# Block probabilities scaled by reciprocal sums: sixteen ScalarE multiplications per tile in place of one GpSimd pass

## The chip, the cores and the metric

The kernel runs on one core of a Trainium2 chip. The metric is the device time of one execution in microseconds (us); less is better. The engines' names in the profile are PE (TensorE; PEld is its weight load), ACT (ScalarE), DVE (VectorE), POOL (GpSimd) and SP (SyncE, which here issues nearly all DMAs).

## What is computed

A transformer layer on x of 2 x 1024 tokens of 256 channels, in fp32: x = layernorm(x + attention(x)), then x = layernorm(x + x Wt + bias), Wt a weight rounded to three levels. The attention has 16 heads of 128 channels and two branches that share one query. Cut to what matters here:

```python
q = rmsnorm(rope(h @ Wq_c @ Wq_up), q_norm_w)            # 16 heads
ck = rmsnorm(h.reshape(b, 64, 16 * 256) @ W_comp, k_norm_w)   # one key (and value) per block of 16 tokens
valid = blk_end[None, :] < pos[:, None]
c_out = softmax([where(valid, q @ ck / sqrt(128), -1e30), sink])[..., :-1] @ ck
s = 50 * tanh(q @ k_sw / sqrt(128) / 50)                 # window of the last 64 tokens
sw_out = softmax([where(window, s, -1e30), sink])[..., :-1] @ v_sw
ao = c_out + sw_out
attention = (ao by 4 groups of heads @ Wg) @ Wo
```

The change is in the normalisation of the block branch: exponentials divided by their sum (the sum takes in the sink).

## The kernel before

**Set-up.** Before the loop the kernel transposes x, makes keys, values and block keys, and multiplies the weights together, so that in the loop the attention's output goes straight from the heads to 256 channels: Weff is Wg times Wo per head (f16, high and low part), and CW is the block values times Weff, 16 heads by 8 blocks = 128 rows to a chunk.

**The loop.** The 2048 tokens are 16 tiles of 128, numbered 0 to 15; a tile is one step `i` of `all_steps` (L339) for its middle part (`mid`). Software pipelining runs four stages in one step: the query of tile i+1 (`front`), the scores and softmax of tile i (`mid`), the output projection and first layernorm of tile i-1 (`proj`), the feed-forward part of tile i-2 (`ffn`). Each engine has its own program of this loop, in an order written out by hand; all ordering between engines is by semaphores. There is no planner. The number of block groups is `groups(i)` = i mod 8 + 1: tile 0 and 8 see 8 blocks at most, tiles 7 and 15 see 64.

**The block probabilities.** For a tile, TensorE writes the block scores of all heads to banks 4 and 5 (L603). VectorE takes the maxima (L1056, `mn`, signal `d_cmax`). ScalarE exponentiates head by head, 16 times (L831), into the tile `Ec` of 128 partitions x (64 blocks x 16 heads), heads innermost, so that one head is a column with a stride of 16 floats; each exponential has its maximum as bias (a pointer to a 128x1 column) and sums its row into `sc` through the accumulator (a second instruction, ACTIVATION_READ_ACCUMULATOR). `Ec` is a part of `room_h`, `sc`, `rc` and `mn` are parts of `room_K`. VectorE's `divide(0)` (the normalisation of the window branch's first half, L1095 to L1114) also takes the reciprocals `rc` of the sums (L1105, signal `d_rc`). GpSimd then multiplies `Ec` by `rc`, one TENSOR_TENSOR over (8 groups - 1) x 16 elements (L1242, signal `g_cn`). TensorE waits for `g_cn` (L690), and at the very end of its step transposes the chunks of `Ec` with `probs_T` (L684, 1 to 8 transposes, signal `p_ct`), after a wait for `d_ql` too (L692). ScalarE copies them out of PSUM to `PcT` (L850, printed at L706 as `room_wo<-PS`, signal `a_ct`), and the next step's `project_blocks` multiplies them with CW (L623).

**The order on each engine, around the change, in one step i with all stages on:**

- TensorE: `queries(i+1)` in two halves, the second one waiting for `a_ct` of the step before (L477); window scores of tile i (L589), which wait for the transposed query by DMA (`s_qt`); x1 transposes (L560); block scores (L599, L603); feed-forward (L568); `project_blocks` (L623) and most of `project_high` (L632); `values(0)` (L666), which waits for GpSimd's mask and for the block exponentials; the rest of L632; `project_low` (L639); `values(1)` (L666); then `probs_T` (L684).
- ScalarE: second square of the query of tile i+1 (L775); four tanh (L816) with a small copy between (`room_h<-PS` at L706); two exponentials of the window branch (L822); 16 block exponentials (L831); the query's high part, twice (`room_K<-PS` at L706), then `output_high(0)` (`ao<-room_wg` at L706); the wait for `p_ct` and the `PcT` copy; the first square of tile i+2 (L775); `output_high(1)` (`ao<-room_wg`).
- VectorE: sums of squares (L1030, L1032), rope (L1045, L1046, L1076), maxima (L1056), query times its norm (L1085), `divide(0)` (L1101, L1105, L1107, L1112), the query's low part twice (L1121, signal `d_ql`), the first layernorm (L1135 to L1147), `divide(1)` (L1101, L1107, L1112).
- GpSimd: a power for the query's norm (L1223), two masks (L1217), the final result of an older tile (L1228), the pass of the change (L1242), `output_low(0)` (L1207), a power and two passes of the first layernorm (L1249, L1253, L1257), `output_low(1)` (L1207).
- SyncE: the queries' transposing DMAs (L370), then the outputs' (L379), high part of both halves before the low part, then the stored result (L397).

On ScalarE, before the change, these lines stand one behind the other:

```python
output_high(0)
act.wait_ge(p_ct, i + 1)
n = groups(i)
narrow(PcT[:, 0:n, :], bank(2, 2)[:, 0:n * P].rearrange("p (a q) -> p a q", q=P), a_ct)
```

Of the kernel before, what the change touches and what calls it, by code (L numbers as in the profile page):

```python
# [8 lines left out]
HEADS, D, QC = 16, 128, 64  # L9
# [4 lines left out]
P = 128  # L14
# [32 lines left out]
def build(nc, h, wqc, wqup, wk, wv, wcomp, qnw, knw, sink, wg, wo, fw, fb, rope_t, block_t, window_t, out):  # L47
# [8 lines left out]
    with ctx:  # L56
# [8 lines left out]
        def sem(name):  # L65
            return ctx.enter_context(nc.semaphore(name))
# [101 lines left out]
        def bank(b, n=1):  # L168
# [28 lines left out]

        a_sq, a_tanh, a_es, a_ec, a_qt, a_ct, a_at, a_xt = (sem(n) for n in (  # L200
            "a_sq", "a_tanh", "a_es", "a_ec", "a_qt", "a_ct", "a_at", "a_xt"))

        d_nq, d_nl, g_rs = sem("d_nq"), sem("d_nl"), sem("g_rs")
        d_red, d_qn, d_rope, d_add, d_cmax, d_rc, d_ql, d_ao, d_fr, d_y, d_xl = (sem(n) for n in (
            "d_red", "d_qn", "d_rope", "d_add", "d_cmax", "d_rc", "d_ql", "d_ao", "d_fr", "d_y", "d_xl"))

        g_mask, g_cn, g_al, g_rl, g_x1, g_xb, g_out = (sem(n) for n in (
            "g_mask", "g_cn", "g_al", "g_rl", "g_x1", "g_xb", "g_out"))
        s_out, s_qt, s_ah, s_al = sem("s_out"), sem("s_qt"), sem("s_ah"), sem("s_al")
        s_chain = sem("s_chain")  # L210

# [17 lines left out]
        def groups(t):  # L229

            return t % TPB + 1
# [170 lines left out]
        def _(pe):  # L402
# [145 lines left out]
            def step(i, front, mid, proj, ffn):  # L548
# [138 lines left out]
                        last.then_inc(p_ct, 1)  # L687

                if mid:
                    pe.wait_ge(g_cn, i + 1)  # L690
                    if front:
                        pe.wait_ge(d_ql, 2 * i + 4)  # L692
                    probs_T(0)
                    probs_T(1)
# [5 lines left out]
        def _(act):  # L700
# [92 lines left out]
            def step(i, front, mid, proj, ffn):  # L793

                def feed_forward_high():

                    act.wait_ge(p_xt, i - 1)
                    narrow(x1T[:, 0, :, :], x1_bank(mid).rearrange("p (k n) -> p k n", k=KC), a_xt)

                if front and i < 1:  # L800
                    square(i + 1, 0)
                if front:
                    square(i + 1, 1)
                if ffn and not mid:
                    feed_forward_high()
                if i == -1:
                    output_weights()
                if i == 0:
                    act.wait_ge(s_fw, 1)
                if mid:  # L810
                    for u, b in enumerate((6, 4, 5, 6)):
                        c, hf = divmod(u, 2)
                        if hf == 0:
                            wait(act, g_mask, 2 * i + c - 1)
                        act.wait_ge(p_sw, 4 * i + u + 1)
                        nc.scalar.activation(E[:, c, 8 * hf:8 * hf + 8, :], bank(b).rearrange("p (a q) -> p a q", q=WIN),  # L816
                                             ACT.Tanh, scale=1.0 / CAP).then_inc(a_tanh, 1)
                        if ffn and u == 0:
                            feed_forward_high()
                    for c in range(2):  # L820
                        act.wait_ge(a_tanh, 4 * i + 2 * c + 2)
                        nc.scalar.activation(E[:, c, :, :], E[:, c, :, :], ACT.Exp, scale=CAP).then_inc(a_es, 1)  # L822
                if mid:
                    if i == 0:
                        evac(G_FT, wfT[:, :, :], two(G_FT))

                    act.wait_ge(d_cmax, i + 1)
                    wait(act, p_ct, i)
                    n = SUB * groups(i)
                    for hd in range(HEADS):  # L830
                        last = nc.scalar.activation(Ec[:, 0:n, hd], bank(4 + hd // 8)[:, (hd % 8) * n:(hd % 8 + 1) * n], ACT.Exp,  # L831
                                                    bias=mn[:, hd:hd + 1], accum_out=sc[:, hd:hd + 1])
                        if hd % 8 == 7:
                            last.then_inc(a_ec, 1)
                if front and i >= 0:
                    query_high(i + 1, 0)
                    query_high(i + 1, 1)
                if i == -1:
                    value_weights(act, lambda dst, src: nc.scalar.mul(dst, src, v_unit), 0)
                if mid:  # L840
                    def output_high(c):

                        act.wait_ge(d_ao, 2 * i + c + 1)
                        wait(act, s_ah, 64 * i)
                        narrow(ao16[:, 0, c, :, :], ao[:, c, :, :], a_at)

                    output_high(0)
                    act.wait_ge(p_ct, i + 1)
                    n = groups(i)
                    narrow(PcT[:, 0:n, :], bank(2, 2)[:, 0:n * P].rearrange("p (a q) -> p a q", q=P), a_ct)  # L850
                    if i + 2 < NT:
                        square(i + 2, 0)
                    output_high(1)
# [5 lines left out]
        def _(dve):  # L859
# [164 lines left out]
            def step(i, front, mid, proj, ffn):  # L1024
# [65 lines left out]
                def divide(c):  # L1090

                    dve.wait_ge(p_pv, 2 * i + c + 1)

                    full = bank(4, 4).rearrange("p (k x) -> p k x", x=1024)[:, :, 0:3 * VW].rearrange("p k (n d) -> p k n d", d=VW)
                    third = bank(5)[:, 0:2 * VW].rearrange("p (n d) -> p n d", d=VW)  # L1095

                    def split(x):
                        return x[:, 0:6].rearrange("p (k n) -> p k n", k=2), x[:, 6:8]

                    for pv, d, e in zip((full[:, :, :, D], third[:, :, D]), split(dn), split(e1)):  # L1100
                        chained(V_.tensor_tensor(d, pv, e, ALU.add))  # L1101
                    if c == 0:
                        dve.wait_ge(a_ec, 2 * i + 2)
                        wait(dve, g_cn, i)
                        V_.reciprocal(rc[:, :], sc[:, :]).then_inc(d_rc, 1)  # L1105
                    after_link()
                    link(V_.reciprocal(r8[:, :], dn[:, :]))  # L1107
                    wait(dve, g_al, 2 * i + c - 1)
                    for o, pv, r in ((ao[:, c, 0:6, :].rearrange("p (k n) d -> p k n d", k=2), full[:, :, :, 0:D],
                                      split(r8)[0].unsqueeze(3).to_broadcast([P, 2, 3, D])),  # L1110
                                     (ao[:, c, 6:8, :], third[:, :, 0:D], split(r8)[1].unsqueeze(2).to_broadcast([P, 2, D]))):
                        last = V_.tensor_tensor(o, pv, r, ALU.mult)  # L1112
                    last.then_inc(d_ao, 1)
                    dve.wait_ge(d_ao, 2 * i + c + 1)  # L1114
# [43 lines left out]
        def _(pool):  # L1158
# [41 lines left out]
            def step(i, front, mid, proj, ffn):  # L1200
# [34 lines left out]
                if mid:  # L1235
                    mask(1)
                    for tile in stored(i):
                        results(tile)
                    pool.wait_ge(d_rc, i + 1)
                    wait(pool, p_ct, i)  # L1240
                    n = SUB * groups(i) - 1
                    G.tensor_tensor(Ec[:, 0:n, :], Ec[:, 0:n, :], rc[:, :].unsqueeze(1).to_broadcast([P, n, HEADS]),  # L1242
                                    ALU.mult).then_inc(g_cn, 1)
                    output_low(0)
                if proj or ffn:

# [41 lines left out]
```

## Time and profile before

| | us |
|---|---|
| median of 3 runs | 418.98 (415.02 to 420.5) |
| the profiled execution, its own time | 418.8 |
| its span | 417.0 |
| PE busy | 366.6 (88% of the span) |
| DVE busy | 327.7 (79%) |
| POOL busy | 302.5 (73%) |
| ACT busy | 285.9 (69%) |

How to read it: the span is from the first to the last instruction of the profiled execution, the 1.8 us around it belong to its time too. Busy shares are averages over the set-up (the first 85 us or so) and the loop. In the loop a tile takes between 18.4 and 21.3 us.

### The profile page before, as it was taken

The numbers are of one execution on the slowest core, as the hardware profiler recorded it, in microseconds if no ns is written. First come the engines' busy times: TensorE is split into PE (matmuls) and PEld (weight loads), VectorE is DVE, ScalarE is ACT, GpSimd is POOL, SyncE is SP. The second block draws the span as 40 slices with busy tenths as digits, with TensorE's granted clock in tenths as the row PEclk, the third lists the DMA queues.
The fourth block names the chain that finished last, engine by engine and source line by source line (L and its number), as shares of the span: only waits on it lengthen the run. The fifth ranks groups of instructions, "written<-read, shape, count | busy, mean of one in ns | idle before, by whom it ended". The sixth has DMA issues, their size and how long they took to land. (4 is left out here: it accounts for less than half of the span.)

```text
span 417.0 us, 8782 instructions
## 1 busy us (share of the span) xinstructions
PE 366.6 (88%) x3109; PEld 296.8 (71%) x3111; DVE 327.7 (79%) x663; ACT 285.9 (69%) x818; POOL 302.5 (73%) x190
## 2 busy tenths in 40 slices
PE   6995797958989889999999999989899999989771
PEld 5994585646859677776868787868677787868650
DVE  3686779677889998898979797999999898943411
ACT  4657764685876969696968595876969696956200
POOL 1845352074797989888979787998989898968615
PEclk9999889988999999999999999999999999999896
DMA  7993002687676775767576758787776757584350
GB/s 251 319 262 110 1 0 24 180 307 139 102 124 117 112 126 92 141 88 140 92 129 85 127 102 124 106 128 136 106 142 100 137 90 134 97 130 63 56 72 26
DMA packets 150285, 50.22 MB, mean 120 GB/s; under 512 B 138592, under 2 KB 148832, under 8 KB 149984
## 3 DMA queue, kind: packets, MB, share of 16 engines
q1 hardware_dynamic: 149424, 49.32, 63.1%
q8 instruction: 25, 0.41, 0.4%
q10 hardware_dynamic: 816, 0.33, 0.3%
q14 instruction: 20, 0.16, 0.1%
HBM read 11.87 MB, written 4.19 MB: 39 GB/s over the span
## 5 line engine op out<-in xcount | busy, mean ns | idle before, releaser
L1207 POOL TENSOR_TENSOR ao<-room_wg,ao 128x1024 f16<-128x1024 f32 x32 | 68.3, 2134 | 17.0 <-ACT ao L706 16.9
L666 PE MATMUL PS<-V,room_wg 128*128 128x129 f32 x512 | 69.0, 286 | 10.8 <-POOL room_wg L1217 4.5
L1217 POOL TENSOR_TENSOR room_wg<-room_comp,keep 128x1024 f32<-128x1024 f32 x32 | 74.7, 2356 | 1.9 <-ACT room_comp L822 1.9
L666 PEld LDWEIGHTS PS<-V,room_wg 128*128 128x128 f32 x512 | 62.7, 197 | 16.0 <-POOL room_wg L1217 7.0
L831 ACT ACTIVATE room_h<-PS,room_K 128x8 f32<-128x8 f32 (+7 forms) x256 | 70.8, 376 | 1.4 <-DVE room_K L1056 1.1
L831 ACT ACTIVATION_READ_ACCUMULATOR room_h<-PS,room_K 128x1 f32 x256 | 63.5, 262 | 0.0
L1223 POOL TENSOR_TENSOR ny<-nx,nu 128x16 f32<-128x16 f32 x16 | 46.7, 2916 | 22.2 <-DVE nx L1032 22.2
L632 PE MATMUL PS<-Weff,aoT 128*128 128x256 f16 x512 | 60.8, 273 | 0.4 <-DMA aoT<-ao 0.4
L632 PEld LDWEIGHTS PS<-Weff,aoT 128*128 128x128 f16 x512 | 49.8, 98 | 8.4 <-DMA aoT<-ao 1.1
L589 PE MATMUL PS<-room_h,kT 128*128 128x512 f16 x192 | 47.6, 380 | 9.2 <-DMA room_h<-room_K 8.3
L1030 DVE TENSOR_REDUCE ssq<-room_wg 128x8 f32<-128x1024 f32 x30 | 36.5, 1219 | 17.3 <-ACT room_wg L775 16.9
L706 ACT ACTIVATE ao<-room_wg 128x1024 f16<-128x1024 f32 x32 | 33.8, 1055 | 17.4 <-DVE room_wg L1112 17.2
L706 ACT ACTIVATE room_wo<-PS 128x128 f32<-128x128 f32 (+7 forms) x16 | 10.4, 652 | 48.6 <-PE PS L684 48.6
L1112 DVE TENSOR_TENSOR room_wg<-PS,r 128x768 f32<-128x768 f32 x64 | 41.2, 685 | 1.1
L477 PE MATMUL PS<-wqup_p,xcT 128*128 128x512 f32 x128 | 36.8, 425 | 5.1 <-POOL wqup_p L1181 4.5
L589 PEld LDWEIGHTS PS<-room_h,kT 128*128 128x128 f16 x192 | 16.8, 98 | 32.5 <-DMA room_h<-room_K 12.5
L1121 DVE TENSOR_TENSOR room_K<-PS,room_K 128x1024 f16<-128x1024 f32 x32 | 37.7, 1217 | 0.5
L1085 DVE TENSOR_TENSOR PS<-PS,ny 128x1024 f32<-128x1024 f32 x32 | 37.6, 1220 | 0.0
L816 ACT ACTIVATE room_comp<-PS 128x512 f32<-128x512 f32 x64 | 35.0, 611 | 0.4 <-PE PS L589 0.4
L706 ACT ACTIVATE room_K<-PS 128x1024 f16<-128x1024 f32 x32 | 33.3, 1075 | 2.6 <-DVE PS L1085 2.2
L623 PE MATMUL PS<-CW,room_wo 128*128 128x256 f32 (+1 forms) x144 | 35.0, 389 | 0.0
L775 ACT ACTIVATE room_wg<-PS 128x1024 f32<-128x1024 f32 x30 | 30.5, 1020 | 5.4 <-PE PS L477 5.2
(181 smaller groups left out, 740.2 us busy)
## 6 DMA issues: line engine op xcount, KB each, us to landing
H<-in_L_attn_h SPq DMA_DIRECT2D x4, 512.0 KB, 6.3
room_wg<-in_L_attn_Wg SPq DMA_DIRECT2D x1, 2048.0 KB, 14.3
cw_rows<-staged SPq DMA_DIRECT2D x1, 2048.0 KB, 6.4
CW<-cw_rows SPq DMA_DIRECT2D x1, 2048.0 KB, 7.8
aoT<-ao SPq DMA_TRANSPOSE x128, 2.7
out<-room_wo SPq DMA_DIRECT2D x16, 128.0 KB, 2.0
CW<-in_L_attn_Wq_up SPq DMA_DIRECT2D x2, 512.0 KB, 13.1
room_wo<-in_L_attn_Wo SPq DMA_DIRECT2D x1, 1024.0 KB, 14.6
```

What stands on the lines that cost most here:

```text
L477: last = nc.tensor.matmul(qbank(hf)[:, (n % 2) * 512:(n % 2 + 1) * 512], xcT[:, t * P:(t + 1) * P], wqup_p[:, w, n * 512:(n + 1) * 512], s ...
L589: last = nc.tensor.matmul(bank(b), kT[:, kp, at + c * WIN:at + c * WIN + P], qT[:, qp, 8 * hf:8 * hf + 8, c * WIN:(c + 1) * WIN], start=n ...
L632: nc.tensor.matmul(o, aoT[:, 0, hd % 2, hd // 2, :], Weff[:, wp, hd, :], start=False, stop=False)
L666: last = nc.tensor.matmul(pv, Pm[:, c, 2 * pr:2 * pr + 2, :], V[:, 2 * i + c, :], start=True, stop=True)
L706: nc.scalar.activation(dst, src, ACT.Copy).then_inc(s, 1)
L831: last = nc.scalar.activation(Ec[:, 0:n, hd], bank(4 + hd // 8)[:, (hd % 8) * n:(hd % 8 + 1) * n], ACT.Exp, bias=mn[:, hd:hd + 1], accum_o ...
L1085: V_.tensor_tensor(by_head(hf), by_head(hf), ny[:, heads].unsqueeze(2).to_broadcast([P, 8, D]), ALU.mult).then_inc(d_qn, 1)
L1112: last = V_.tensor_tensor(o, pv, r, ALU.mult)
L1121: V_.tensor_tensor(qp[:, 1, heads, :], by_head(hf), qp[:, 0, heads, :], ALU.subtract).then_inc(d_ql, 1)
L1207: G.tensor_tensor(ao16[:, 1, c, :, :], ao[:, c, :, :], ao16[:, 0, c, :, :], ALU.subtract).then_inc(g_al, 1)
L1217: G.tensor_tensor(Pm[:, c, :, :], E[:, c, :, :], keep[:, :, :], ALU.mult).then_inc(g_mask, 1)
L1223: G.tensor_tensor(ny[:, 0:HEADS], nx[:, 0:HEADS], nu[:, 0:HEADS], ALU.pow).then_inc(g_rs, 1)
```

## The change

ScalarE takes over the multiplication by the reciprocals. Behind `output_high(0)` it waits for `d_rc` and issues 16 multiplications, one per head, in place in `Ec`, with the head's column of `rc` as scale (a pointer to a 128x1 column) over 8 groups - 1 elements with a stride of 16 floats. The last of them signals `a_cn`, which takes the place of `g_cn` in TensorE's wait ahead of `probs_T` and in VectorE's wait ahead of the next reciprocals. GpSimd's pass and its two waits go. Everything else stands where it stood.

```diff
@@ TensorE
                 if mid:
-                    pe.wait_ge(g_cn, i + 1)
+                    pe.wait_ge(a_cn, i + 1)
                     if front:
                         pe.wait_ge(d_ql, 2 * i + 4)
                     probs_T(0)
@@ ScalarE
                     output_high(0)
+                    act.wait_ge(d_rc, i + 1)
+                    n = SUB * groups(i) - 1
+                    for hd in range(HEADS):
+                        last = nc.scalar.mul(Ec[:, 0:n, hd], Ec[:, 0:n, hd], rc[:, hd:hd + 1])
+                    last.then_inc(a_cn, 1)
                     act.wait_ge(p_ct, i + 1)
                     n = groups(i)
                     narrow(PcT[:, 0:n, :], bank(2, 2)[:, 0:n * P].rearrange("p (a q) -> p a q", q=P), a_ct)
@@ VectorE
                     if c == 0:
                         dve.wait_ge(a_ec, 2 * i + 2)
-                        wait(dve, g_cn, i)
+                        wait(dve, a_cn, i)
                         V_.reciprocal(rc[:, :], sc[:, :]).then_inc(d_rc, 1)
@@ GpSimd
                     for tile in stored(i):
                         results(tile)
-                    pool.wait_ge(d_rc, i + 1)
-                    wait(pool, p_ct, i)
-                    n = SUB * groups(i) - 1
-                    G.tensor_tensor(Ec[:, 0:n, :], Ec[:, 0:n, :], rc[:, :].unsqueeze(1).to_broadcast([P, n, HEADS]),
-                                    ALU.mult).then_inc(g_cn, 1)
                     output_low(0)
```

## Rows read from the trace of the kernel before

**Rows 1.** The page, part 1: busy us, share of the span, instructions, by engine.

```profile
PE 366.6 (88%) x3109; PEld 296.8 (71%) x3111; DVE 327.7 (79%) x663; ACT 285.9 (69%) x818; POOL 302.5 (73%) x190
```

**Rows 2.** Waits, whole run: who waited for whom, us, times, longest.

```profile
ACT room_wo L706 <- PE PS L684: 48.6, 16, 4.6
```

**Rows 3.** Line L1242 by itself: length ns min/median/max, first and last start; its waiters.

```profile
L1242 POOL TENSOR_TENSOR room_h<-room_h,room_K x16: 420/1377/2330, 93.2 to 383.2; 128x112 f32<-128x112 f32 x2, 128x240 f32<-128x240 f32 x2, 128x368 f32<-128x368 f32 x2, 128x496 f32<-128x496 f32 x2
...
who waited for it (us, times):
```

**Rows 4.** Timeline, tile 2: start us, length us, engine, line; idle before, releaser.

```profile
131.51 1.06 ACT L706 ACTIVATE ao<-room_wg 128x1024 f16<-128x1024 f32 x1 [0.92 <-DVE room_wg L1112]
131.51 2.35 DVE L1121 TENSOR_TENSOR room_K<-PS,room_K 128x1024 f16<-128x1024 f32 x2
...
133.98 0.31 PEld L684 LDWEIGHTS PS<-ident,room_h 128*128 128x128 f32 x3
...
134.56 0.49 ACT L706 ACTIVATE room_wo<-PS 128x384 f32<-128x384 f32 x1 [2.00 <-PE PS L684]
...
135.50 1.02 ACT L775 ACTIVATE room_wg<-PS 128x1024 f32<-128x1024 f32 x1 [0.44 <-PE PS L477]
...
136.93 1.06 ACT L706 ACTIVATE ao<-room_wg 128x1024 f16<-128x1024 f32 x1 [0.40 <-DVE room_wg L1112]
...
137.43 1.47 PE L589 MATMUL PS<-room_h,kT 128*128 128x512 f16 x6 [1.05 <-DMA room_h<-room_K]
137.89 1.01 ACT L775 ACTIVATE room_wg<-PS 128x1024 f32<-128x1024 f32 x1
...
138.79 0.59 ACT L816 ACTIVATE room_comp<-PS 128x512 f32<-128x512 f32 x1
```

**Rows 5.** Timeline, from tile 2 to tile 3: what the squares and tanh lead to.

```profile
143.32 4.67 POOL L1217 TENSOR_TENSOR room_wg<-room_comp,keep 128x1024 f32<-128x1024 f32 x2
...
145.73 2.37 PE L666 MATMUL PS<-V,room_wg 128*128 128x129 f32 x16
...
149.96 1.06 ACT L706 ACTIVATE ao<-room_wg 128x1024 f16<-128x1024 f32 x1 [0.71 <-DVE room_wg L1112]
```

**Rows 6.** Timeline, ACT alone: the PcT copies of tiles 0, 1, 4, 6, 7, 8, 15.

```profile
97.87 0.28 ACT L706 ACTIVATE room_wo<-PS 128x128 f32<-128x128 f32 x1 [2.26 <-PE PS L684]
...
115.93 0.39 ACT L706 ACTIVATE room_wo<-PS 128x256 f32<-128x256 f32 x1 [1.89 <-PE PS L684]
...
172.97 0.71 ACT L706 ACTIVATE room_wo<-PS 128x640 f32<-128x640 f32 x1 [2.84 <-PE PS L684]
...
213.16 0.92 ACT L706 ACTIVATE room_wo<-PS 128x896 f32<-128x896 f32 x1 [4.04 <-PE PS L684]
...
234.71 1.03 ACT L706 ACTIVATE room_wo<-PS 128x1024 f32<-128x1024 f32 x1 [4.31 <-PE PS L684]
...
254.58 0.28 ACT L706 ACTIVATE room_wo<-PS 128x128 f32<-128x128 f32 x1 [4.26 <-PE PS L684]
...
389.94 1.02 ACT L706 ACTIVATE room_wo<-PS 128x1024 f32<-128x1024 f32 x1 [4.59 <-PE PS L684]
```

**Rows 7.** Timeline, PE weight loads: the transposes of tile 7.

```profile
233.53 0.91 PEld L684 LDWEIGHTS PS<-ident,room_h 128*128 128x128 f32 x8
```

**Rows 8.** Timeline, ACT alone: a copy scaled by a pointer; block exponentials of tile 7.

```profile
44.38 0.69 ACT L758 ACTIVATE kT<-PS,wqk 128x512 f16<-128x512 f32 x1 [1.04 <-PE PS L491]
44.97 1.05 ACT L730 ACTIVATE keep<-room_wo 128x1024 f32<-128x1024 f32 x1
...
221.90 0.36 ACT L831 ACTIVATE room_h<-PS,room_K 128x64 f32<-128x64 f32 x1
222.09 0.20 ACT L831 ACTIVATION_READ_ACCUMULATOR room_h<-PS,room_K 128x1 f32 x1
222.18 0.37 ACT L831 ACTIVATE room_h<-PS,room_K 128x64 f32<-128x64 f32 x1
```

More of the change, by code:

```diff
@@ L196, in build @@
             "p_q", "p_sw", "p_cs", "p_o", "p_pv", "p_ct", "p_xt", "p_f"))
-        a_sq, a_tanh, a_es, a_ec, a_qt, a_ct, a_at, a_xt = (sem(n) for n in (
-            "a_sq", "a_tanh", "a_es", "a_ec", "a_qt", "a_ct", "a_at", "a_xt"))
+        a_sq, a_tanh, a_es, a_ec, a_qt, a_ct, a_at, a_xt, a_cn = (sem(n) for n in (
+            "a_sq", "a_tanh", "a_es", "a_ec", "a_qt", "a_ct", "a_at", "a_xt", "a_cn"))
         d_nq, d_nl, g_rs = sem("d_nq"), sem("d_nl"), sem("g_rs")
@@ L205, in build @@
             "d_red", "d_qn", "d_rope", "d_add", "d_cmax", "d_rc", "d_ql", "d_ao", "d_fr", "d_y", "d_xl"))
-        g_mask, g_cn, g_al, g_rl, g_x1, g_xb, g_out = (sem(n) for n in (
-            "g_mask", "g_cn", "g_al", "g_rl", "g_x1", "g_xb", "g_out"))
+        g_mask, g_al, g_rl, g_x1, g_xb, g_out = (sem(n) for n in (
+            "g_mask", "g_al", "g_rl", "g_x1", "g_xb", "g_out"))
         s_out, s_qt, s_ah, s_al = sem("s_out"), sem("s_qt"), sem("s_ah"), sem("s_al")
```

## The prediction, made before the changed kernel ran

> **What bounds the kernel now.** I read the page first: PE is busy for 88% of the span, POOL for 73%, ACT for 69% [rows 1]. By these shares the change looks harmless or good: it takes work from the third engine and gives it to the least loaded one. A share doesn't say where in a tile the work lies, so I read the waits next. ACT's longest wait is the one before the `PcT` copy, for TensorE's transposes L684: 48.6 us in 16 waits, 3.0 us a tile [rows 2]. The new copies go into exactly this hole. Then the line L1242 alone: the pass takes 0.42 to 2.33 us, and nobody's idle time ended with it [rows 3]. So TensorE never waited for GpSimd's product. What is removed cost nothing, and the question is only whether ACT gives the product as early as TensorE wants it.
>
> For that the timeline of one tile is needed [rows 4]. In tile 2 `output_high(0)` ends at 131.51 + 1.06 = 132.57. TensorE starts the transposes at 133.98, right behind VectorE's second L1121 (131.51 + 2.35 = 133.86), which it waits for through `d_ql`. So TensorE wants the product 1.41 us after `output_high(0)` ends. In tile 7 it has a longer list of block products to work through, and starts at 233.53 [rows 7].
>
> Last, who feels it when the transposes are late. TensorE is in order: `queries(i+2)` stand behind them, the first square (L775) needs these, and from the `PcT` copy on ACT runs almost without a gap to the first tanh: 134.56, 135.50 (0.44 of waiting for TensorE itself), 136.93 (0.40 idle), 137.89, 138.79 [rows 4]. The squares and tanh lead to GpSimd's mask, to `values(0)`, to `divide(0)` and to the next `output_high(0)`, which waits 0.71 us for it [rows 5], and so to the next transposes. This is a ring, with one turn per tile, and the 0.40 us before `output_high(1)` is the only slack I find in it on ACT in tile 2. TensorE's own wait of 1.05 us for the DMA of the transposed queries (L589) is slack of TensorE's branch, but the tanh behind it comes from ACT's branch: the first scores, three of the six matmuls in 1.47 us, are there at 137.43 + 0.74 = 138.17, and the tanh starts 0.62 later, when the square is out of the way.
>
> **The price of one multiplication.** The trace has no small copy from SBUF scaled by a pointer. The nearest row is L758: 128x512 with a pointer as scale, from PSUM, 0.69 us long, the next instruction 0.59 behind it, so two neighbours overlap by 0.10 [rows 8]. The slope is read from the `PcT` copies: 1.03 us at 1024 elements against 0.28 at 128, 0.84 ns an element [rows 6]. At 63 elements that gives 0.59 - 449 x 0.00084 = 0.21 us from start to start, at 7 elements 0.17. The block exponentials, with a pointer too, are followed by their accumulator read after 0.19 us at 64 elements [rows 8], a bit less than 0.21. A source in SBUF seems to cost some more: from `output_high(1)` to the next start 0.96 us, from the square out of PSUM 0.90, both of 1024 elements [rows 4]. I take 0.18 us at 7 elements and 0.23 at 63, near the PSUM rows plus half of that difference. Lower bound: the exponentials' 0.19 at 64, so 0.145 at 8. Upper bound: a full pair of exponential and read, 222.18 - 221.90 = 0.28 at 64 [rows 8], so 0.235 at 8.
>
> The Trainium skill has a price for the same thing ("ScalarE: Activation LUTs", What ACT_TABLE_LOAD costs): 280 ns + 0.833 ns per element for an ACTIVATE with one pointer operand, with an overlap of about 93 ns back to back. By it an estimate of the pitch is 0.19 us at 7 and 0.24 at 63 elements; the forecast below would then be some 2.5 us higher.
>
> **From there to the lateness.** Per tile: the first of the 16 starts 0.10 before `output_high(0)` ends, 15 pitches follow, the last takes its length (0.69 less 0.42 at 7 elements: 0.27; 0.32 at 63), and the handover to TensorE is put at 0.1. At one group: 15 x 0.18 + 0.27 - 0.10 + 0.1 = 2.97 us after the end of `output_high(0)`. At eight: 15 x 0.23 + 0.32 = 3.77. That is 2.97 + 0.114 (g - 1) for g groups. From the transposes' start to the copy it takes 134.56 - 133.98 = 0.58 at three groups [rows 4] and 234.71 - 233.53 = 1.18 at eight [rows 6, 7], so 0.34 + 0.12 (g - 1). The sum, 3.31 + 0.234 (g - 1), is the new idle-plus-work time ahead of the `PcT` copy. The old one is the idle time X in its row. The difference is how late TensorE starts the transposes:
>
> g = 1 (tile 0): 3.31 - 2.26 = 1.05. g = 2: 3.54 - 1.89 = 1.65. g = 3: 3.78 - 2.00 = 1.78. g = 4: 4.01 - 2.42 = 1.59. g = 5: 4.25 - 2.84 = 1.41. g = 6: 4.48 - 3.44 = 1.04. g = 7: 4.71 - 4.04 = 0.67. g = 8 (tile 7): 4.95 - 4.31 = 0.64 (X from [rows 4, 6]; for four and six groups, which have no row, it is put in the middle of its neighbours). Tiles 0 to 7 together: 9.83 us. Tile 8 has X = 4.26, more than 3.31: no delay. Tiles 9 to 14 repeat tiles 1 to 6 within 0.05 us: 8.14. Tile 15: 4.95 - 4.59 = 0.36. Gross 18.3 us.
>
> Off this goes the ring's slack: the 0.40 us of tile 2 and of the three tiles like it (1, 9, 10), and some 0.2 us in tiles 3 and 12, 2.0 us in all. Net 16.3 us.
>
> **The other edits.** `act.wait_ge(d_rc)` costs nothing: the reciprocals stand ahead of L1112, which `output_high(0)` has waited for; this is the work that hides it. Behind the copies in ACT's queue stand the `PcT` copy, a square and `output_high(1)`; the copy could not start earlier anyway, the other two are in the count because they hang on TensorE. VectorE's wait for `a_cn` is for the tile before, some 15 us old. GpSimd's pass gone brings `output_low(0)` forward by up to about a microsecond where the pass ended behind `output_high(0)`, but its DMAs queue on SyncE behind those of `output_high(1)`, so this is worth 0; if something did hang on it, at most the pass's own length, 22 us over 16 tiles by 16 x 1.38 [rows 3], is the bound on the side of a gain. It is excluded for nearly all of it by the empty list of waiters. No DMA is added or moved.
>
> The Trainium skill speaks of another gain ("SBUF — State Buffer", SBUF: two separate sides): GpSimd and VectorE share a port pair, and a VectorE instruction with two SBUF inputs, or in a two-port mode, and a GpSimd one block each other. No VectorE instruction beside the pass reads two large inputs from SBUF (L1112 and L1121 read PSUM), so the sum keeps 0 for it.
>
> **Sum.** 418.8 (the profiled execution) + 16.3 = 435.1; against the median of 418.98 the base differs by 0.2. Forecast 435 us, 4% slower.
>
> **The rivals.**
> A, *dear copies*: the pointer or the 64-byte stride in SBUF makes the multiplications run at the pair's rate, 0.235 to 0.28. Per tile (15 x 0.055 or 15 x 0.05) some 0.8 us more; 14 tiles already late, tile 8 still not: 11 us more, 446. For it: the exponentials get longer within a tile, so ACT takes instructions in faster than it finishes them. Against it: a pair is two instructions. Chance 0.13.
> B, *the DMA wait swallows part*: the ring of the small tiles goes through the scores and not the squares, so the 1.05 us of L589 is slack instead of the 0.40. Tiles 1 to 3 and 9 to 11 then lose 2 x (0.60 + 0.73 + 0.54) = 3.7 us in place of about 8.4. Time 430.4. For it: the wait is in the trace. Against it: tanh starts 0.62 later than its scores. Chance 0.15.
> C, *not slower*: the copies go through at so small a pitch that they fit into the hole. Each 0.01 us of pitch is 15 x 14 x 0.01 = 2.1 us over the 14 late tiles; at 0.037 below my values (0.145 and 0.19, the lower bound itself) 7.8 us go and the loss is 8.5, and from there down the result is within 2%. At 0.10, the accumulator reads' pitch (222.18 - 222.09) [rows 8], the product is there after about 1.7 us, and 419 to 421 us come out. For it: the exponential row stands at just this bound. Against it: L758, and the SBUF source. Chance 0.09.
> D, *GpSimd's relief counts*: `output_low(0)` or the layernorm passes behind it release something on the ring; with cheap copies on top, some microseconds of gain. Chance 0.02; time about 415.
>
> **How the numbers follow.** Forecast 0.61, A 0.13, B 0.15, C 0.09, D 0.02. The range 427 to 443 takes in B, the lower bound of the pitch (427.3) and pitches of up to 0.038 above mine; it leaves out most of A, C and D, some 0.2. Faster by over 2% (a measurement of this kernel can tell about 2% from no change, here 8.4 us) 0.01, within 2% 0.10, slower by over 2% 0.89.
>
> **What the changed profile would show.** The wait of ACT for L684 falls from 48.6 us by the copies' time, 16 x 16 x 0.2 = 52 us of issue, so it shrinks to the transposes themselves, about 14 us with the handover; TensorE gets a new wait before L684, released by the new ACT line, of 1 to 1.8 us in tiles 1 to 5 and 9 to 13, under 0.8 in tiles 6, 7, 14 and 15 and none in tile 8. The copies start 0.18 to 0.23 us apart. The idle time before `output_high(1)` in tiles 1, 2, 9 and 10 goes to zero, L589's wait for the DMA falls below 0.3 us in the small tiles, and POOL is busy for 22 us less. Tile 8 keeps its distance to tile 9's start, within 0.3 us. The forecast is wrong if the wait before L684 is there but the tiles are no longer by it (the ring has slack elsewhere), if the pitch is outside 0.145 to 0.28, or if the tiles grow by more than the wait, which would point to TensorE's clock or to another queue.

## The result and the profile after

| | before | after |
|---|---|---|
| median, us | 417.58 (415.02 to 420.5, 4 runs) | 438.88 (437.74 to 442.13, 4 runs) |
| the profiled execution, its span | 418.8, 417.0 | 439.15, 437.4 |

The ratio is 1.052, with a 95% interval of 1.0425 to 1.0616: 21.3 us slower. The forecast was 435 us, 427 to 443. Some executions of a kernel are slower than its others, in two cases far slower (784 us in e5_held, 2019 us in e7_dense): the medians count them, the ratios and their intervals don't.

First the page of after, part 1, in the columns of [rows 1].

```profile
PE 375.6 (86%) x3109; PEld 300.8 (69%) x3111; DVE 325.9 (75%) x663; ACT 346.1 (79%) x1074; POOL 281.9 (64%) x174
```

ACT has 60 us more of busy time (285.9 before) and POOL 20.6 less. No engine is nearer to full than PE, and PE's share fell. The shares alone would not tell why the kernel is slower. The waits of after do:

```profile
POOL ao L1212 <- ACT ao L706: 64.6, 32, 5.2
DVE ssq L1035 <- ACT room_wg L775: 42.1, 29, 3.1
PEld PS L684 <- ACT room_h L851: 28.3, 15, 2.5
PE PS L684 <- ACT room_h L851: 25.4, 15, 2.3
...
ACT room_wo L706 <- PE PS L684: 14.0, 16, 1.2
```

ACT's wait for the transposes went from 48.6 us [rows 2] to 14.0, which is the transposes themselves. In its place TensorE waits 25.4 us, in 15 of the 16 tiles, for L851, the new multiplications. The 42.1 us of VectorE are the same delay one step further on: it waits for the squares, 16.9 us before. The first line, 64.6 us, is GpSimd's idle time before `output_low`, 16.9 before. A part of it comes from the missing pass alone (38.6 us in e1_no_pass below, at the time of before).

The timeline of tile 2 in after, to be laid beside [rows 4]:

```profile
131.32 1.06 ACT L706 ACTIVATE ao<-room_wg 128x1024 f16<-128x1024 f32 x1 [0.90 <-DVE room_wg L1117]
131.32 2.36 DVE L1126 TENSOR_TENSOR room_K<-PS,room_K 128x1024 f16<-128x1024 f32 x2
...
132.28 3.66 ACT L851 ACTIVATE room_h<-room_h,room_K 128x23 f32<-128x23 f32 x16
...
135.99 0.50 PEld L684 LDWEIGHTS PS<-ident,room_h 128*128 128x128 f32 x3 [2.33 <-ACT room_h L851]
...
136.55 3.42 PE L477 MATMUL PS<-wqup_p,xcT 128*128 128x512 f32 x8
136.93 0.49 ACT L706 ACTIVATE room_wo<-PS 128x384 f32<-128x384 f32 x1 [0.99 <-PE PS L684]
...
138.64 1.03 ACT L775 ACTIVATE room_wg<-PS 128x1024 f32<-128x1024 f32 x1 [1.22 <-PE PS L477]
139.56 1.05 ACT L706 ACTIVATE ao<-room_wg 128x1024 f16<-128x1024 f32 x1
...
139.81 1.47 PE L589 MATMUL PS<-room_h,kT 128*128 128x512 f16 x6
...
141.41 0.60 ACT L816 ACTIVATE room_comp<-PS 128x512 f32<-128x512 f32 x1
```

Up to the end of `output_high(0)` the two look the same. Then 16 copies take 3.66 us, and the transposes start 3.61 us after that end instead of 1.41. ACT waits 1.22 us for the queries (L477) where it waited 0.44: they take 3.42 us, and before

```profile
134.28 2.10 PE L477 MATMUL PS<-wqup_p,xcT 128*128 128x512 f32 x8
```

That is TensorE's clock, which e4_warm below is about. From the square to the first tanh there is no gap left on ACT, and L589 starts without a wait for the DMA. Tile 7 is the case with the longest copies, 63 elements:

```profile
238.67 1.06 ACT L706 ACTIVATE ao<-room_wg 128x1024 f16<-128x1024 f32 x1 [1.08 <-DVE room_wg L1117]
239.64 4.74 ACT L851 ACTIVATE room_h<-room_h,room_K 128x63 f32<-128x63 f32 x16
245.56 1.03 ACT L706 ACTIVATE room_wo<-PS 128x1024 f32<-128x1024 f32 x1 [1.18 <-PE PS L684]
```

**The account of the 20.4 us between the two spans.** I read the distance from the end of `output_high(0)` to the first transpose for all 16 tiles in both traces. It grows by 1.6, 2.0, 2.2, 2.2, 2.1, 1.8, 1.5, 1.6 us in tiles 0 to 7, not at all in tile 8, and by 2.0, 2.2, 2.2, 2.0, 1.8, 1.5, 1.3 us in tiles 9 to 15: 28.0 us of lateness. From the `PcT` copy of tile 0 to that of tile 15 the loop takes 292.1 us before and 315.4 after, 23.3 us more; with tile 0's own 1.6 us, 24.9. So 3.1 us were taken up on balance, and that balance hides two terms: by e4_warm below some 2.7 us of a lower clock were added, and some 5.8 us taken up by slack. The set-up of this execution of after was 4.2 us shorter, the drain behind tile 15 0.4 us. Set-ups vary by about that: the end of tile 0's `output_high(0)` lies between 91.6 and 97.3 us in the profiled executions. The stretch between the `PcT` copies of tiles 0 and 15, called the loop below, is therefore a finer measure than the time: 292.1 us in before, 292.6 in e1_no_pass, 292.3 in e6_split.

### The profile page after: what moved, and what is told of

It reads as the page before. It is cut to its first block and busy times, and to the rows that moved or that the text cites. A ratio compares the mean times of both kernels' runs of the same rounds, so it can differ in the third digit from the quotient of the medians.

```text
span 437.4 us, 9007 instructions
## 1 busy us (share of the span) xinstructions
PE 375.6 (86%) x3109; PEld 300.8 (69%) x3111; DVE 325.9 (75%) x663; ACT 346.1 (79%) x1074; POOL 281.9 (64%) x174
## 5 line engine op out<-in xcount | busy, mean ns | idle before, releaser
L1212 POOL TENSOR_TENSOR ao<-room_wg,ao 128x1024 f16<-128x1024 f32 x32 | 68.3, 2134 | 64.6 <-ACT ao L706 64.6
L666 PE MATMUL PS<-V,room_wg 128*128 128x129 f32 x512 | 69.1, 286 | 10.7 <-POOL room_wg L1222 4.5
L666 PEld LDWEIGHTS PS<-V,room_wg 128*128 128x128 f32 x512 | 62.7, 197 | 16.4 <-POOL room_wg L1222 7.7
L1035 DVE TENSOR_REDUCE ssq<-room_wg 128x8 f32<-128x1024 f32 x30 | 36.5, 1220 | 42.1 <-ACT room_wg L775 42.1
L831 ACT ACTIVATION_READ_ACCUMULATOR room_h<-PS,room_K 128x1 f32 x256 | 64.8, 276 | 0.0
L851 ACT ACTIVATE room_h<-room_h,room_K 128x7 f32<-128x7 f32 (+7 forms) x256 | 63.8, 340 | 0.0
L589 PE MATMUL PS<-room_h,kT 128*128 128x512 f16 x192 | 48.6, 382 | 2.1 <-ACT room_comp L816 1.8
L477 PE MATMUL PS<-wqup_p,xcT 128*128 128x512 f32 x128 | 40.0, 454 | 2.4 <-POOL wqup_p L1186 1.8
L623 PE MATMUL PS<-CW,room_wo 128*128 128x256 f32 (+1 forms) x144 | 36.3, 400 | 0.0
L589 PEld LDWEIGHTS PS<-room_h,kT 128*128 128x128 f16 x192 | 16.4, 98 | 25.9 <-ACT room_comp L816 8.4
## 6 DMA issues: line engine op xcount, KB each, us to landing
room_wg<-in_L_attn_Wg SPq DMA_DIRECT2D x1, 2048.0 KB, 12.3
```

Of the source, the lines that this page charges most:

```text
L477: last = nc.tensor.matmul(qbank(hf)[:, (n % 2) * 512:(n % 2 + 1) * 512], xcT[:, t * P:(t + 1) * P], wqup_p[:, w, n * 512:(n + 1) * 512], s ...
L589: last = nc.tensor.matmul(bank(b), kT[:, kp, at + c * WIN:at + c * WIN + P], qT[:, qp, 8 * hf:8 * hf + 8, c * WIN:(c + 1) * WIN], start=n ...
L666: last = nc.tensor.matmul(pv, Pm[:, c, 2 * pr:2 * pr + 2, :], V[:, 2 * i + c, :], start=True, stop=True)
L851: last = nc.scalar.mul(Ec[:, 0:n, hd], Ec[:, 0:n, hd], rc[:, hd:hd + 1])
L1212: G.tensor_tensor(ao16[:, 1, c, :, :], ao[:, c, :, :], ao16[:, 0, c, :, :], ALU.subtract).then_inc(g_al, 1)
```

## The experiments

The theory to be tested: the removed pass cost nothing, and TensorE's late start of L684 is the whole loss. The rivals: ACT's added load by itself, GpSimd's part, the clock. All ratios are to the kernel before on the same chip, with medians of before of 417.3 (e1 to e4), 418.0 (e5 to e8) and 417.7 us (e9, e10).

**e1_no_pass.** After without the copies; TensorE waits for the reciprocals.

```diff
-                    for hd in range(HEADS):
-                        last = nc.scalar.mul(Ec[:, 0:n, hd], Ec[:, 0:n, hd], rc[:, hd:hd + 1])
-                    last.then_inc(a_cn, 1)
...
-                    pe.wait_ge(a_cn, i + 1)
+                    pe.wait_ge(d_rc, i + 1)
```

> The kernel of after without the 16 copies on ScalarE and without GpSimd's pass; TensorE waits for the reciprocals alone. The normalisation of the block branch is left out. Theory (the copies make the product late, the pass cost nothing): the tiles go by as in the kernel before, gap from the end of output_high(0) to the transposes 1.4 us in the small tiles, time within 2 us of before (416 to 420). Rival 1 (GpSimd's pass was on the ring for a part after all): 3 us or more under before. Rival 2 (something else that the change moved costs the time, not the copies): it stays above 425.

417.51 us, ratio 0.999 (0.9954 to 1.0025). Neither the pass nor anything else in the change but the copies makes a difference that the time shows. This is also the most that any cheaper way of this multiplication could bring: by the interval 2 us at best.

**e2_beside.** The kernel before, with the 16 multiplications on ScalarE besides, in a dead area.

```diff
                     output_high(0)
+                    act.wait_ge(d_rc, i + 1)
...
+                    for hd in range(HEADS):
+                        last = nc.scalar.mul(scr[:, 0:n, hd], scr[:, 0:n, hd], rc[:, hd:hd + 1])
+                    last.then_inc(a_cn, 1)
```

> The kernel before, GpSimd's pass and TensorE's wait for it kept, and on top of it the 16 multiplications on ScalarE at the place of the change, in an area that nobody reads. ScalarE is as busy as after, the product is as early as before. Theory (most of the loss is TensorE's late start, the rest ScalarE's own queue): no wait of TensorE before L684; the PcT copy comes late by the length of the copies less its old idle time, 0.3 to 1.5 us a tile, partly taken up by the 0.2 to 0.5 us before the square; in all 7 to 12 us over before (425 to 430). Rival (ScalarE's load is the whole loss): 436 to 441, as after. Rival (the product's lateness is the whole loss): 416 to 420.

423.27 us, ratio 1.0119 (1.006 to 1.0178): 5.0 us (2.5 to 7.4), mostly under the 7 to 12 that I expected. The waits show where it comes in:

```profile
PE PS L478 <- ACT room_wo L707: 11.1, 12, 1.2
```

TensorE doesn't wait before the transposes: their distance from `output_high(0)` is that of before in every tile, within 0.1 us. It waits for the late `PcT` copy ahead of the second half of the queries. So with the same load on ScalarE but the product in time, 5.0 of the 21.3 us are there. Load alone is not the loss.

**e3_early.** After, with the copies ahead of `output_high(0)`.

```diff
-                    output_high(0)
                     act.wait_ge(d_rc, i + 1)
                     n = SUB * groups(i) - 1
                     for hd in range(HEADS):
                         last = nc.scalar.mul(Ec[:, 0:n, hd], Ec[:, 0:n, hd], rc[:, hd:hd + 1])
                     last.then_inc(a_cn, 1)
+                    output_high(0)
```

> After, with the wait for the reciprocals and the 16 copies ahead of output_high(0) instead of behind it. ScalarE does the same work. Theory (lateness): the product is ready some 1.8 us earlier, within 0.5 us of the old start of the transposes in tiles 1 to 5 and 9 to 13 and in time in the others; TensorE's wait before L684 falls from 25 us to 2 to 5 us, time 2 to 6 us over before (419 to 424). Rival (ScalarE's occupied time itself costs, wherever it stands): above 430. Rival (output_high(0) late by 2 to 4 us makes the output's transposing DMAs late): L639's wait for the DMA grows to over 0.5 us a tile and the time is 425 to 430.

436.55 us, ratio 1.0419 (1.0364 to 1.0475). A miss: I had expected 419 to 424. The product is now in time (TensorE waits 0.2 to 0.7 us in six tiles and not in the others), yet the loss is nearly all there, and neither rival is right in its mechanism. The waits name another queue:

```profile
POOL ao L1212 <- ACT ao L706: 81.3, 17, 6.3
...
PEld PS L560 <- POOL room_wo L1253: 18.6, 13, 3.9
```

and GpSimd's timeline in tile 2 shows it:

```profile
133.33 2.14 POOL L1212 TENSOR_TENSOR ao<-room_wg,ao 128x1024 f16<-128x1024 f32 x1 [5.63 <-ACT ao L706]
135.43 0.69 POOL L1249 TENSOR_TENSOR ny<-nx,nu 128x2 f32<-128x2 f32 x1
136.23 1.21 POOL L1253 TENSOR_SCALAR room_wo<-room_wo,mv,ny 128x256 f32<-128x256 f32 x1
137.53 0.73 POOL L1257 TENSOR_TENSOR room_h<-room_wo,fb_s 128x256 f32<-128x256 f32 x1
138.21 2.15 POOL L1212 TENSOR_TENSOR ao<-room_wg,ao 128x1024 f16<-128x1024 f32 x1
140.32 2.91 POOL L1228 TENSOR_TENSOR ny<-nx,nu 128x16 f32<-128x16 f32 x1
```

In before, GpSimd had gaps at the same place:

```profile
132.64 2.13 POOL L1207 TENSOR_TENSOR ao<-room_wg,ao 128x1024 f16<-128x1024 f32 x1 [1.52 <-ACT ao L706]
135.28 0.70 POOL L1249 TENSOR_TENSOR ny<-nx,nu 128x2 f32<-128x2 f32 x1 [0.50 <-DVE nx L1147]
...
140.44 2.92 POOL L1223 TENSOR_TENSOR ny<-nx,nu 128x16 f32<-128x16 f32 x1 [0.22 <-DVE nx L1032]
```

`output_high(0)` now ends at 133.25 and GpSimd's `output_low(0)` stands behind it. Before the change it ran in a hole that GpSimd had there; now the five GpSimd instructions behind it follow without a gap, x1 comes late to L560 (TensorE's weight loads waited 5.2 us for it in before), and the power and masks of the next tile come late too: `values` (L666) waits 13.7 us in all for GpSimd's masks, 4.5 in before. e9 tests this.

**e4_warm.** After, with TensorE's wait filled by transposes of the identity.

```diff
-                    pe.wait_ge(a_cn, i + 1)
                     if front:
                         pe.wait_ge(d_ql, 2 * i + 4)
+                        for _ in range(0 if i == 8 else (8, 17, 16, 14, 12, 11, 9, 9)[groups(i) - 1]):
+                            nc.tensor.transpose(bank(2)[:, 0:P], ident[:, :], ident[:, :])
+                    pe.wait_ge(a_cn, i + 1)
```

> After, with 8 to 17 transposes of the identity per tile on TensorE, ahead of its wait for the copies, into the bank that the real transposes overwrite; none in tiles 8 and 15. They fill the wait and are shorter than it. Theory (the copies are late; the lower granted clock in tiles 0 to 3 is a by-product worth 1 to 3 us): granted clock at full level through the loop, time 1 to 4 us under after (435 to 438), the gap from output_high(0) to the transposes unchanged within 0.1 us. Rival (the clock is a large part of the loss, TensorE's pauses let it fall): 6 us or more under after. Rival (the clock plays no part): within 0.5 us of after.

439.59 us, ratio 1.0522 (1.0481 to 1.0563), against 1.052 (1.0425 to 1.0616) for after: no gain, but the two intervals leave room for one of 4 us, so the times don't decide. Stretches of after, then of e4_warm; the number behind POOL's is the granted clock, as a share of 2.4 GHz:

```profile
90.00:130.00 40.00, 34.77 (x298) 27.22 (x299) 31.30 (x62) 34.82 (x123) 26.12 (x13) 0.87 0.62 104
130.00:170.00 40.00, 35.62 (x314) 27.77 (x313) 32.96 (x65) 35.07 (x122) 29.09 (x17) 0.96 0.62 107
```

```profile
90.00:130.00 40.00, 36.22 (x314) 29.05 (x314) 30.88 (x61) 33.12 (x122) 25.03 (x13) 0.89 0.69 120
130.00:170.00 40.00, 38.62 (x354) 30.60 (x353) 34.02 (x70) 36.32 (x122) 29.70 (x18) 1.00 0.69 104
```

In after the granted clock was 0.50 from 116 to 118 us and 0.51 from 136 to 138, that is 1.2 GHz, each time behind TensorE's wait of 2.3 and 2.1 us for the copies (tile 2's transposes and queries took 0.90 and 3.42 us in place of 0.52 and 2.10). In before it was 1.00 from 110 to 170 us, and with TensorE kept busy it was so in e4_warm too. The traces show what this was worth. From one `PcT` copy to the next, e4_warm is 0.5, 1.4 and 0.8 us shorter than after between tiles 0 and 3, and equal within 0.03 us between all later ones; the lateness of the transposes is the same within 0.03 us in all tiles but the first. So the clock cost some 2.7 us in after, within my 1 to 3. In the time of e4_warm it is hidden: tile 0's eight transposes of the identity ran at the low clock and outlasted the wait, so the real ones came 0.9 us later than in after, and the set-up of the profiled execution was longer.

**e5_held.** The kernel before, TensorE alone held up by as much as it waited in after.

```diff
                         pe.wait_ge(d_ql, 2 * i + 4)
+                        for _ in range(0 if i == 8 else (14, 22, 20, 18, 16, 14, 12, 12)[groups(i) - 1]):
+                            nc.tensor.transpose(bank(2)[:, 0:P], ident[:, :], ident[:, :])
```

> The kernel before, GpSimd's pass kept and no copy on ScalarE; TensorE alone is held up ahead of the real transposes, by 12 to 22 transposes of the identity, 0.11 us each, about as long as it waited per tile in the profile of after (1.3 to 2.5 us, none in tiles 8 and 15; 24 us in all). Theory (what costs is TensorE starting L684 late, by nearly its full amount): 17 to 22 us over before (434 to 440), the idle time before output_high(1) gone, the DMA wait of L589 under 0.3 us. Rival (the ring has slack on TensorE's side, the 1.05 us of L589's DMA wait): 8 to 13 us over before. Rival (TensorE's delay is swallowed, ScalarE's queue is the cost): under 4 us.

Ratio 1.0396 (1.0312 to 1.0481), or 16.6 us (13.0 to 20.1), with the executions compared between 433.73 and 437.65; the profiled one is the one of 784 us, so no rows are shown and its lateness is not measured. An estimate: the 115 transposes of e10_held_half below made TensorE 13.7 us late, so these 230 make some 27, near the 28.0 of after. Without one copy on ScalarE, and with GpSimd's pass in place, most of the loss is there. It is just under the 17 to 22 that I expected, with an interval that reaches into them. That TensorE's lateness is the whole of the 21.3 us is not shown: 2.7 of the rest are the clock, which e10_held_half, with half of these transposes, held at 1.00 from 110 to 275 us, and the other 2 are within the noise.

**e6_split.** Eight heads on ScalarE, eight in one GpSimd pass.

```diff
-                    for hd in range(HEADS):
+                    for hd in range(8):
...
+                    G.tensor_tensor(Ec[:, 0:n, 8:], Ec[:, 0:n, 8:], rc[:, 8:].unsqueeze(1).to_broadcast([P, n, 8]),
+                                    ALU.mult).then_inc(g_cn, 1)
```

> After, with 8 heads scaled on ScalarE at the place of the change and the other 8 by one GpSimd pass of half the length at its old place. Both are waited for. Theory (lateness beyond the old gap is all that costs): the 8 copies take 1.6 to 2.4 us, so TensorE waits 0.1 to 0.4 us in tiles 1 to 4 and 9 to 12 and nowhere else: 1 to 4 us over before (418 to 421). Rival (each copy on ScalarE costs its own length, the loss is proportional to their number): half of the loss, 10 to 11 us over before (427 to 429).

416.96 us, ratio 0.9979 (0.9943 to 1.0016): as before, and just under the 418 to 421 that I expected. Half of the copies cost nothing, not half of the loss. The line L852 of this kernel, the eight copies, by itself:

```profile
who waited for it (us, times):
  PEld PS L684: 3.8, 7
  PE PS L684: 2.4, 5
```

The transposes start 2.2 us later in sum over the 16 tiles, and the loop is 0.2 us longer. So the cost is a threshold per tile and not a price per copy.

**e7_dense.** The 16 copies on elements side by side instead of every 16th.

```diff
-                        last = nc.scalar.mul(Ec[:, 0:n, hd], Ec[:, 0:n, hd], rc[:, hd:hd + 1])
+                        piece = room_h[:, 3072 + n * hd:3072 + n * hd + n]
+                        last = nc.scalar.mul(piece, piece, rc[:, hd:hd + 1])
```

> After, with each of the 16 copies on 8 groups - 1 elements that lie side by side in the same area, instead of every 16th float; the reciprocals thus fall on other elements (the normalisation of the block branch is changed). Same number, size and pointer. Theory (the step of 1.7 ns an element from 7 to 63 elements in after, twice the 0.84 of other rows, is the 64-byte stride of the source in SBUF): 16 copies of 63 take 4.0 us and not 4.7, those of 7 still 3.2; the time 4 to 7 us under after (432 to 435). Rival (the slope has nothing to do with the layout, it is the in-place form, the fp32 source or the queue): 4.7 us and the same time as after.

433.26 us, ratio 1.0323 (1.0249 to 1.0397), about 8 us under after where I expected 4 to 7. The profiled execution is the one of 2019 us: TensorE's instructions are far longer in it, but the lengths on ACT can be read. Groups by line and form: busy us, mean ns of one; first after, then e7_dense, the longest and the shortest copies.

```profile
L851 ACT ACTIVATE room_h<-room_h,room_K 128x63 f32<-128x63 f32 x32 | 9.5, 387 | 0.0
...
L851 ACT ACTIVATE room_h<-room_h,room_K 128x7 f32<-128x7 f32 x32 | 6.5, 294 | 0.0
```

```profile
L852 ACT ACTIVATE room_h<-room_h,room_K 128x63 f32<-128x63 f32 x32 | 7.8, 333 | 0.0
...
L852 ACT ACTIVATE room_h<-room_h,room_K 128x7 f32<-128x7 f32 x32 | 6.3, 286 | 0.0
```

Strided, (387 - 294) / 56 = 1.7 ns an element; side by side, (333 - 286) / 56 = 0.84. The stride of 64 bytes doubles the price of an element, and 16 such copies of 63 elements cost some 0.8 us more. The edit moves source and destination together, so it doesn't say by itself which of the two pays.

**e8_imm.** The copies with a constant as scale.

```diff
-                        last = nc.scalar.mul(Ec[:, 0:n, hd], Ec[:, 0:n, hd], rc[:, hd:hd + 1])
+                        last = nc.scalar.mul(Ec[:, 0:n, hd], Ec[:, 0:n, hd], 0.5)
```

> After, with the constant 0.5 as scale of the 16 copies in place of the pointer to the reciprocal (the normalisation of the block branch is left out). Same number, size and stride. Theory (a pointer adds about 0.09 us to the length and to the pitch): 16 copies take 1.4 us less (1.8 us at 7 elements, 3.3 us at 63), TensorE's wait before L684 falls from 25 us to about 6, time 421 to 426. Rival (the pitch is set by the elements and a fixed cost, the pointer's fetch overlaps): 3.2 to 4.7 us as in after, and its time.

419.01 us, ratio 1.0048 (1.0008 to 1.0089); the time is below the 421 to 426 that I expected, the rows as expected:

```profile
L851 ACT ACTIVATE room_h<-room_h 128x63 f32<-128x63 f32 x32 | 6.6, 296 | 0.0
...
L851 ACT ACTIVATE room_h<-room_h 128x7 f32<-128x7 f32 x32 | 3.5, 200 | 0.0
```

A pointer adds 0.09 us to each copy (387 to 296, 294 to 200). The 16 copies take 1.75 us at 7 elements and 3.29 at 63, in place of 3.23 and 4.74. Taking the pointers away takes nine tenths of the loss away: the lateness falls from 28.0 to 7.0 us, and a good part of the rest is taken up by slack.

**e9_early_light.** e3_early, with `output_low(0)` on GpSimd cut to an eighth.

```diff
-                    G.tensor_tensor(ao16[:, 1, c, :, :], ao[:, c, :, :], ao16[:, 0, c, :, :], ALU.subtract).then_inc(g_al, 1)
+                    a = slice(0, 1 if c == 0 < i else PAIRS)
+                    G.tensor_tensor(ao16[:, 1, c, a, :], ao[:, c, a, :], ao16[:, 0, c, a, :], ALU.subtract).then_inc(g_al, 1)
```

> e3_early (copies ahead of output_high(0)), with output_low(0) on GpSimd cut to one of its eight pairs of heads from tile 1 on (0.4 us in place of 2.1; the rest of the low part of the first half keeps tile 0's values, so that part of the output's correction is left out). Theory for e3's 19 us (output_high(0) ends 2 to 3 us later, GpSimd's output_low(0) behind it runs into the first layernorm's passes, x1 comes late to TensorE's L560, and the power and the masks of the next tile with it): the wait of L560 for GpSimd falls from 18.6 us to under 5, time 418 to 424. Rival (ScalarE is what is full: the copies take 3.2 to 4.7 us out of a hole of 2 to 4.3, wherever they stand): above 430 still. Rival (the transposing DMAs of the high part start late and TensorE waits for them): 428 to 436, with a DMA wait at L632.

418.96 us, ratio 1.0025 (0.9984 to 1.0066), from 1.0419. The waits:

```profile
PEld PS L560 <- POOL room_wo L1254: 5.4, 2, 3.9
```

18.6 us in 13 times became 5.4 in two, and the wait of L666 for the masks is 5.2 us. ScalarE still does `output_high(0)` and all 16 copies in one piece. So what cost 17 us in e3_early was one GpSimd instruction of 2.1 us that had been pushed out of GpSimd's hole, and ScalarE was never full. What the cut of `output_low(0)` would bring to the kernel before, by itself, wasn't run.

**e10_held_half.** e5_held with half as many transposes, (7, 11, 10, 9, 8, 7, 6, 6).

> e5_held with half as many transposes of the identity (6 to 11 a tile, 0.7 to 1.2 us, none in tiles 8 and 15; some 12 us in all). Theory (nearly every microsecond of TensorE's lateness beyond a slack of 0.4 us in four of the small tiles is paid): 8 to 12 us over before (426 to 430). Rival (there is a threshold of about 1 us per tile from the DMA wait of L589): 0 to 5 us over before.

427.39 us, ratio 1.0237 (1.0152 to 1.0322), so 9.9 us (6.3 to 13.4). ACT's wait for the transposes:

```profile
ACT room_wo L708 <- PE PS L684: 62.5, 16, 5.0
```

62.5 - 48.6 [rows 2] = 13.9 us of lateness for 9.9 us of time. Beside it stand after, 28.0 us of lateness for 21.3, and e8_imm, where the distances of the 16 tiles grew by 7.0 us in sum, for 2.0 (0.48% of 418). In all three the time is the lateness less 4 to 7 us. The loop says the same with less noise. Without tile 0's own lateness, e8_imm has 6.2 us of it for a loop 3.6 us longer, e10_held_half 12.3 for 8.6, and e4_warm, whose clock was 1.00 from 110 us on, 26.6 for 20.7: 2.6, 3.7 and 5.9 us are taken up on balance. That is the shape of the theory, with a slack larger than my 2.0 us.

## Why the prediction was right, and where its terms were off

- **What bounds the kernel, and that the removed pass is worth 0:** right. It stood in the empty list of waiters [rows 3], and e1_no_pass measured it.
- **The copies fill ACT's hole and the product comes late:** right. The new wait of TensorE is there in 15 tiles and not in tile 8, and from tile 8's transposes to the end of tile 9's `output_high(0)` it is 16.13 us before and after. POOL lost 20.6 us of work where I had said 22. L589's wait for the DMA went, and the idle time before `output_high(1)` in the small tiles too.
- **The lateness, 18.3 us gross: mis-sized, 28.0.** The term that was mis-sized is the pitch; with it the distance from `output_high(0)` to the transposes came out 0.2 us too short in tile 0 and 0.9 in tile 7, 9.0 of the 9.7 us in sum. I had 0.18 us at 7 elements and 0.23 at 63; measured are (3.23 - 0.29) / 15 = 0.196 and (4.74 - 0.39) / 15 = 0.29. The second is even outside my bounds of 0.145 to 0.28. I had carried a slope of 0.84 ns an element from rows whose source lies side by side over to a source with a stride of 16 floats; e7_dense shows 0.84 and 1.7 for the two. The exponentials [rows 8] write with this stride and don't pay for it, which misled me: from one of them to its accumulator read it is 0.150 us at 8 elements and 0.198 at 64, 0.86 ns an element, out of PSUM. So it is the source in SBUF that differs, by elimination: no run has a strided source with a dense destination. The Trainium skill speaks of it ("SBUF — State Buffer", Door 1: The DMA port swizzle): SBUF has lines of 16 bytes, and each access that crosses to a new line pays a penalty. The rows of after and e7_dense agree with it (1.7 against 0.84 ns); the exponentials' 0.86 shows no such penalty on ScalarE's destination.
- **The pointer's price in the Trainium skill** ("ScalarE: Activation LUTs", What ACT_TABLE_LOAD costs; 93 ns for a pointer, a pitch of 0.19 at 7 elements): the trace agrees, with 94 and 91 ns in e8_imm and 0.196 us. Its 0.24 at 63 is too low here, for the stride; side by side, in e7_dense, it is 0.238.
- **The slack, 2.0 us: too small.** With the clock out of the way (e4_warm) 5.9 us of lateness were taken up in the loop. Of these 1.3 are at its end: from tile 14's `PcT` copy to tile 15's it takes as long as before, since behind tile 14 there are no more queries and squares to be late. The rest, 0.3 to 0.8 us a tile, lies between tiles 0 and 4 and between tiles 9 and 13. Which wait gives it can't be placed from these runs.
- **The clock: put at nothing, 2.7.** The prediction named its sign, tiles that grow by more than the wait, and the sign came: from tile 0 to tile 3 the loop grew by 7.3 us for 6.4 of lateness.
- **The number came out in part by luck.** 28.0 + 2.7 - 5.8 = 24.9 us, against 18.3 - 2.0 = 16.3. The profiled execution of after gave 4.5 of the 24.9 back by its shorter set-up and drain; the medians differ by 21.3. The lateness of 28.0 is nearer to rival A's 29.3 than to my 18.3. The pitch at 63 elements, 0.29, was by the prediction's own words a sign that the forecast is wrong. The path and the sign of the change were right, the sizes along it were not.
- **Rival A** (dear copies) was half right: the copies were dear by the stride, not by the pair's rate. **B** (the DMA wait of 1.05 us is slack) fell in its size: e10_held_half would then have been 0 to 5 us over before and was 9.9. The slack of 0.3 to 0.8 us a tile lies between B's 1.05 and my 0.40. (B's "about 8.4" is 2 x 5.02 less the slack of tiles 1, 2, 3, 9 and 10, 1.8, so 8.2.) **C** needs a smaller pitch; without the pointer it is 0.10 us at 7 elements and 0.20 at 63 (e8_imm). **D** fell with e1_no_pass.
- **Where the theory had a hole** was not in the forecast but in e3_early: I followed the late product and forgot that the moved instructions delay `output_high(0)`, whose reader on GpSimd is in order with half of the next tile. The prediction's check of `output_low(0)` asked only whether it would gain by coming earlier, never what it costs to come later.

None of the kernels beats the one before beyond the noise. e6_split equals it (0.9979, interval over 1), and by e1_no_pass there is next to nothing to be had from this multiplication.

## What to carry to other kernels

An idle hole of 3 us in an engine's tile is no room for 3 us of work on the path of another engine: what counts is when the consumer asks for the product, here 1.4 us after the hole opens in the small tiles. Read for each consumer the distance from the hole's start to its first use, and for each producer that the new work delays, what else stands behind its reader in that reader's queue. A pass of one instruction on a slow engine can be better than 16 short ones on a fast one; price these with their pointer (0.09 us each) and with the stride of their source, and move only as many as fit (8 of 16 were free here).

## What the runs showed of the hardware

- ScalarE's copies in place with a stride of 64 bytes in SBUF cost twice as much per element as those side by side (fp32, 1.7 against 0.84 ns, after and e7_dense), while a destination with the same stride, with the source in PSUM, cost 0.86 (the exponentials of before). That it is the source that pays follows from these two, not from a run of its own.
- A pointer as scale adds 0.09 us to each ScalarE instruction, and it isn't hidden behind the one before: 16 of them took 1.48 us longer at 7 elements (3.23 against 1.75).
- The granted clock was 0.50 and 0.51, 1.2 GHz, in two stretches of 2 us of after, behind waits of TensorE of 2.3 and 2.1 us in tiles 1 and 2. Behind waits as long in tiles 9 and 10 the same queries took 2.1 us, as at full clock. Kept busy over these waits (e4_warm), TensorE ran at 1.00, and the first three tiles were 2.7 us shorter.
